# The turn of x's norm moved between the two tiles of the first key and value products

## The reference, cut to what matters

```python
def _L0_xattn_ref(x, y, Wq, bq, Wk, bk, Wv, bv, Wkv_dca, bkv_dca, ...):
    y_dca = y[:, -DCA:, :]               # last 16 context rows of a batch
    y_main = y[:, :-DCA, :]              # the other 48
    kv_dca = (y_dca @ Wkv_dca + bkv_dca).reshape(b, DCA, 2, H, HD)
    q = _ln((x @ Wq + bq).reshape(b, s1, H, HD), qn_w, qn_b)
    kv = jnp.concatenate([y_main @ Wk + bk, y_main @ Wv + bv], axis=-1)
    ...
    k = _ln(kv[..., :HD], kn_w, kn_b)
    v = kv[..., HD:]
    ...
    return ctx @ Wo + bo

x = x + jnp.tanh(g_xattn[0]) * _L0_xattn_ref(_layernorm(x, axis=-1), ctx_1024, ...)
```

## Time and profile before

| | us |
|---|---|
| median of 3 runs | 406.82 (404.75 to 408.09) |
| the profiled execution's own time | 408.39 |
| its span, first to last instruction | 406.3 |
| TensorE busy in it | 378.1 (93%) |
| VectorE busy | 312.0 (77%) |
| ScalarE busy | 194.1 (48%) |
| GpSimd busy | 171.6 (42%) |

### The profile page before, as it was taken

The page is one execution under the profiler, slowest core; times in us unless marked ns, Lnnn a source line. Parts: engine busy times, 40 slices in busy tenths (PEclk is TensorE's granted clock), DMA queues, the critical chain, the costliest instruction groups (busy, mean ns, idle before and its releaser), DMA issues. The chain is left out here.

```text
span 406.3 us, 8983 instructions
## 1 busy us (share of the span) xinstructions
PE 378.1 (93%) x3594; PEld 353.3 (87%) x3594; DVE 312.0 (77%) x709; ACT 194.1 (48%) x401; POOL 171.6 (42%) x208
## 2 busy tenths in 40 slices
PE   0989999979999999899999999999999998999996
PEld 0877878868899989899999898999989998999996
DVE  3888877787787686775688988899899798965553
ACT  3577676742624344244256625554654555333232
POOL 4146646341313212223165444556524864642332
PEclk9999998999999999999999999999999999999999
DMA  7902102030000300300200020010001000000000
GB/s 213 337 12 77 59 26 78 15 119 3 0 2 0 128 5 1 131 0 2 81 0 2 2 67 2 2 57 11 2 0 56 3 0 2 0 2 27 27 27 27
DMA packets 7165, 16.32 MB, mean 40 GB/s; under 512 B 1218, under 2 KB 4803, under 8 KB 6740
## 3 DMA queue, kind: packets, MB, share of 16 engines
q1 hardware_dynamic: 7124, 15.75, 11.4%
HBM read 14.70 MB, written 1.05 MB: 39 GB/s over the span
## 5 line engine op out<-in xcount | busy, mean ns | idle before, releaser
L1715 POOL TENSOR_SCALAR work<-work,lut_step,lut 128x344 f32<-128x344 int32 (+1 forms) x60 | 42.2, 716 | 52.2 <-DVE work L1634 50.6
L312 PE MATMUL ps<-wB_hi,workr 128*128 128x256 f32 x224 | 50.8, 292 | 2.8 <-POOL workr L1297 1.8
L312 PE MATMUL ps<-xT_hi,wB_hi 128*128 128x256 f32 x176 | 51.3, 292 | 1.8 <-DVE work L1166 1.6
L1297 POOL TENSOR_TENSOR workr<-work,workr 128x256 fp32r<-128x256 f32 (+1 forms) x36 | 23.0, 638 | 63.2 <-ACT workr L1098 63.2
L312 PE MATMUL ps<-xT_lo,wB_hi 128*128 128x256 f32 x176 | 49.7, 282 | 0.0
L312 PE MATMUL ps<-xT_hi,wB_lo 128*128 128x256 f32 x176 | 49.6, 282 | 0.0
L312 PE MATMUL ps<-wN_hi,shared_r 128*128 128x256 f32 x256 | 47.9, 281 | 0.0
L1649 DVE COPY_PREDICATED work<-work 128x1376 f32<-128x1376 int32 (+5 forms) x36 | 42.0, 1167 | 2.2
L312 PEld LDWEIGHTS ps<-wB_hi,workr 128*128 128x128 f32 x224 | 38.2, 189 | 5.8 <-issue 3.3
L312 PEld LDWEIGHTS ps<-wN_hi,shared_r 128*128 128x128 f32 x256 | 40.2, 188 | 0.4 <-DVE shared_r L1611 0.3
L312 PE MATMUL ps<-xT_hi,wM_hi 128*128 128x256 f32 x128 | 36.6, 286 | 2.2 <-ACT work L1474 2.2
(11 more groups left out here) (219 smaller groups left out, 1099.8 us busy)
## 6 DMA issues: line engine op xcount, KB each, us to landing
stage<-in_wC SPq DMA_DIRECT2D x3, 1280.0 KB, 6.7
stage<-in_wB SPq DMA_DIRECT2D x4, 768.0 KB, 4.5
stage<-in_idx SPq DMA_DIRECT2D x4, 536.0 KB, 3.4
work<-in_wC SPq DMA_DIRECT2D x2, 640.0 KB, 7.1
stage<-in_wA SPq DMA_DIRECT2D x2, 512.0 KB, 5.3
out<-x SPq DMA_DIRECT2D x8, 128.0 KB, 1.8
x<-in_x SPq DMA_DIRECT2D x2, 256.0 KB, 4.7
x<-in_x SPq DMA_DIRECT2D x1, 512.0 KB, 9.1
```

The costliest lines, as they stand in the source:

```text
L312: last = nc.tensor.matmul(out, l, r, start=start and i == 0, stop=stop and i == 2)
L1297: nc.gpsimd.tensor_tensor(h_lo[k % 3][0:n], h3[k % 3][0:n], h_hi[k % 3][0:n].bitcast(F32), ALU.subtract).then_inc(*Bp["h_lo"].up())
L1715: nc.gpsimd.tensor_scalar(lev[:, j, 0:n], bits[:, 0, 0:n], lut_step[:, j:j + 1], lut[:, 2 * j:2 * j + 1], ALU.mult, ALU.add).then_inc(*C[" ...
```

## The change

On TensorE the turn of the first norm of x goes from ahead of the key and value products to between their first tile and their second, and the one `keep_warm` product behind the turn goes. On VectorE the statistics of x stay where they are, but the writing of xn goes behind the lower parts of the weights and the context, whose own order is swapped too.

```diff
         def pe_A_start(pe):
             pe.wait_ge(wA_hi_ready, 1)
             keep_warm(5, 0)
-            front_pe(pe, 0, FRONT_A)
-            keep_warm(1, 0)
             pe.wait_ge(wA_lo_ready, 1)
             pe.wait_ge(wv_lo_ready, 1)
             for t in range(TILES):
                 pe_A_kv_main(pe, 0, t)
                 pe_A_kv_last(pe, t)
+                if t == 0:
+                    front_pe(pe, 0, FRONT_A)
             pe_A_q_main(pe, 0)
             pe.wait_ge(bias_lo_ready, 1)
...
             dve.wait_ge(x0_in, 16)
-            front_dve(dve, 0, 0)
-            dve.wait_ge(ctxT0_in, 16)
-            dve.wait_ge(setup_pool, 4)
-            dve_A_ctx(dve, 0)
+            front_stats(dve, 0, 0)
             dve.wait_ge(wA_hi_ready, 1)
             nc.vector.tensor_tensor(wA_lo[:, 0:NWC], ...).then_inc(wA_lo_ready, 1)
...
             nc.vector.tensor_tensor(wA_lo[:, r], ...).then_inc(wv_lo_ready, 1)
+            dve.wait_ge(ctxT0_in, 16)
+            dve.wait_ge(setup_pool, 4)
+            dve_A_ctx(dve, 0)
+            front_norm(dve, 0, 0)
             front_lower(dve, 0, FRONT_A)
             dve.wait_ge(vec_in, 16 * 5)
```

## The result

The changed kernel takes 410.04 us (median of 15 runs, 407.99 to 411.62), the kernel before 407.55 us (median of 15). The ratio is 1.0069, with a 95% interval of 1.0049 to 1.0089: the change makes the kernel slower by 2.8 us, between 2.0 and 3.6. The ratio leaves out three executions of the kernel before, at 411 to 413 us, that stand over 1.5% above its fastest and count as slow; the two medians of all runs lie 2.5 us apart. The profiled execution took 410.55 us, with a span of 408.4 (before: 408.39 and 406.3).

A forecast was written before the change was run, and what follows sets the result against it. L369 was taken as the bounding point, reached by TensorE's products and a VectorE path from L298 to L808. Its 2.2 us delay, passed whole, took the median from 406.82 to 409.0 us, range 405.2 to 411.2.

The forecast's parts named there:

- The place and the mechanism: Start: products begin 1.49 us earlier, but the turn 2.84 us later delays L298, L808 and so L369.
- the bounds: Start of L369: later by 0.5 to 2.8 us, depending on when the clock rises.
- the 2.2 us: L369 starts at 20.70 instead of 18.48, and this delay reaches the kernel's end whole.
- the fall of the clock as a rival of 0.07: Idling ahead of L369 lets the clock fall: slower by more than 1%, 412.7 us; chance 0.07.
- a price of 3.7 us: Extra time if the 24 products of the next weights, behind L369, run at 1.2 GHz.
- My sum: Whole kernel: 2.2 us slower, profiled execution 408.39 to 410.6, median 406.82 to 409.0.
- the start value: Median of the kernel before, 406.82 us from three runs, to which the forecast added 2.2 us.
- That nothing later takes the shift: Behind L369: nothing up to the phase's end waits for a transfer issued at the start, so 2.2 us pass whole.
- Rival (c): Start and 60 us on: L369 isn't held up, the half-clock stretch doesn't recur, 405.0 us; chance 0.03.
- rival (a): Whole kernel: the shift is lost or never comes, median unchanged at 406.8 +- 0.7 us; chance 0.12.

The follow-up runs named there:

- the filled kernel: The changed kernel with eight unread 512-column products between the queries and the wait for the biases ahead of L369; ratios to the kernel before 1.0079 and 1.0060.
- e2: First comparison of the filled kernel, the changed kernel with eight unread products ahead of L369; ratio to the kernel before 1.0079.
- e3: Only VectorE's half of the change, with TensorE's order kept as in the kernel before; ratio to the kernel before 1.0008.
- e4: Only TensorE's half of the change, with VectorE's order kept as in the kernel before; ratio to the kernel before 1.0121.
- e5: Changed kernel, bias centring and second group's statistics ahead of L298, four upper key and value products replacing three warm-up products; ratio to the kernel before 1.0026.
- e9: The changed kernel with only the centring of the biases moved ahead of L298 on VectorE; ratio to the kernel before 1.0030.

## Why the prediction was right, and where it wasn't

**The place and the mechanism** are as forecast. Products at 11.63: they came at 11.43, 11.68 and 11.54 in the three profiles. The turn at 14.35: 13.74, 14.38 and 14.24. VectorE idling 3.9 us ahead of L298: 3.07, 3.78 and 3.70, released by L294. TensorE idling 2.4 us ahead of L369, released by L809: 2.09, 2.10 and 2.09. L369 at 20.70: 19.58, 20.55 and 20.33. In the first profile the clock rose earlier (its six L312 take 2.48 us, those of the others 2.90), and L369 is 0.75 to 0.97 us ahead of the others', 0.11 to 0.25 of it because the products started earlier. That is the lower side of the bounds, and they hold. The shift of L369 was sized at 2.2 us and measures 20.15 - 18.27 = 1.9 as the mean of the profiles.

**The step that failed** is the one that let the 2.2 us through unchanged, with the fall of the clock as a rival of 0.07: "For it, the longest pause in the rows is shorter than the new one". That sentence was the right one to follow. In the profiles the fall is the rule. I gave it a price of 3.7 us, as if all 24 products stayed at half speed and all of it reached L401, and thought it rare. It is frequent and cheaper. Only L644 and a piece of L647 were slow, 3.2 us instead of 1.95 and 2.4 at most instead of 1.89, and 0.56 us of that were covered by TensorE's pause ahead of L401, which is gone in the changed kernel. What is left is 5.95 - 5.00 = 0.95 us, from L369 to L401.

**The sum then.** L401 moves by 26.10 - 23.26 = 2.84 us in the mean of the profiles: 1.89 of VectorE's queue and 0.95 of the clock. The timed ratio says 2.8. My sum said 2.2, from 0.3 us too much on the queue and nothing on the clock. The split rests on five profiles. The timed comparison with the filled kernel can't confirm the 0.95, since its intervals are 1.2 to 1.5 us wide on either side.

**Where luck helped.** The profiled execution took 410.55 us and L401 came at 25.51, against a forecast of 410.6 and 25.6. Two errors cancel there: L369 came 1.1 us earlier than forecast, and the fall of the clock, which the sum had at nothing, gave back nearly as much. Of the 1.04 us by which the median of 410.04 stands above the forecast of 409.0, 0.73 lie in the start value, 406.82 from three runs against 407.55 from fifteen. And the prediction took about 1% for the least that a measurement of this kernel can tell; the interval of fifteen runs is 0.2% wide on either side, and told 0.7% from no change.

**That nothing later takes the shift** held in the profiles. Over the five profiles whose mean clock was 1.0 (e2, e3, e4, e5, e9), L401 starts anywhere from 22.02 to 27.33, and the rest of the span is 381.1, 380.9, 381.1, 381.6 and 381.6 us.

**Rival (c) and rival (a)** fell, since the interval leaves out 1. The Trainium skill (TensorE: Matmul & The Clock Gate, Why this matters for your kernels) asks for no idle gap above about 3 us, so it would allow a gap of this size. Here the clock fell behind 2.09 and 2.10 us of idling in three profiles of three, so the measurement decides against the rule as a safe limit.

## What to carry to other kernels

Earlier work on one engine is worth what the last path into the next common point lets through. Ask what stands behind each wait in the queue that is moved: here 3.0 us of centring and statistics (15.61 to 18.57) that needed nothing from the turn stood behind the one instruction that did. Reordering that queue took the whole loss away, and put too much ahead of that instruction for the next version. And price a new pause on TensorE twice, for its length and for the products behind it at half the clock, less what they were waiting for anyway.

## What the runs showed of the hardware

The clock's rise moved more than I had thought: the same first six L312, started at about 11.5 us behind five warm-up products, took from 2.48 to 2.90 us, and in one profile (e4) the second six still took 2.67. Between the changed kernel's profiles that alone moves L369 by up to 0.97 - 0.25 = 0.7 us. And falls of the clock come in other places without any edit. In the second profile of the kernel before, four unread products of 512 columns that take 1.20 us elsewhere take 2.00:

```profile
27.59 2.00 PE L631 MATMUL ps<-shared_r 128*128 128x512 f32 x4
29.39 1.48 PE L312 MATMUL ps<-shared_r,workAr 128*128 128x512 f32 x3
```

All five profiles of either kernel have such a fall somewhere behind L401, in three of them between 60 and 68 us and in two between 27 and 34. They leave 381.9 to 383.0 us from L401 to the end, where the profiles with a full clock leave 380.9 to 381.6.
